# Words of the relation sums' slots made while the digits are counted; target one-hots of four slots made by one operation

## The reference

```
x = x + mean over 50000 edges (src -> dst, sorted by dst) of (norm(x) @ W + b)[src]      # neighbours
x = x + experts(norm(x)), gated by attention over 32768 other edges (4 heads, 4 experts)
x = x + relu(sum over the same 50000 edges of norm(x)[src] @ weight[relation] * edge_weight)  # relations
x = x + mixture of 8 experts, with a last layer norm
```

## Time and profile before

| what | value |
|---|---|
| median of three runs | 2875.92 us |
| profiled execution, its own time | 2869.64 us |
| its span, first to last instruction | 2867.9 us |
| mean granted TensorE clock (1 is full speed) | 0.776 |
| TensorE matmul busy | 1749.4 us, 61% |
| VectorE busy | 1312.6 us, 46% |
| GpSimd busy | 1063.5 us, 37% |
| ScalarE busy | 711.2 us, 25% |

### The profile page before, as it was taken

How to read it: one execution, slowest core, us unless ns; L and a number is a source line. 1 busy time by engine, 2 the same in 40 slices (tenths; PEclk the granted TensorE clock), 3 DMA queues, 4 the chain that set the end, 5 groups by cost and what they waited for, 6 DMA issues and landing times. The chain is left out here.

```text
span 2867.9 us, 36329 instructions
## 1 busy us (share of the span) xinstructions
PE 1749.4 (61%) x8770; PEld 1356.0 (47%) x8771; DVE 1312.6 (46%) x3820; ACT 711.2 (25%) x1568; POOL 1063.5 (37%) x1102
## 2 busy tenths in 40 slices
PE   3565577677781212399983514544555556799798
PEld 2343355455560101277762414444444446688576
DVE  7476776677740000013245604544555547522534
ACT  0001255555320000023313602222222224100222
POOL 2366555665057777200011174444444441000000
PEclk9776687877895555699986756767777768999899
DMA  4122333333221101022231632333223332233101
GB/s 151 57 73 83 85 101 102 103 105 95 59 24 25 9 8 24 20 74 94 80 122 33 195 97 78 113 97 94 88 88 95 109 96 64 88 137 113 34 1 45
DMA packets 164842, 226.19 MB, mean 79 GB/s; under 512 B 35636, under 2 KB 123990, under 8 KB 161942
## 3 DMA queue, kind: packets, MB, share of 16 engines
q0 software_dynamic: 47392, 105.58, 13.6%
q1 hardware_dynamic: 114048, 116.08, 12.9%
q10 hardware_dynamic: 3318, 3.50, 0.4%
HBM read 172.48 MB, written 105.03 MB: 97 GB/s over the span
## 5 line engine op out<-in xcount | busy, mean ns | idle before, releaser
L2018 PE MATMUL part<-coef,held 128*128 128x128 f32 x2368 | 414.1, 331 | 438.2 <-DVE window_sums L2040 188.8
L2018 PEld LDWEIGHTS part<-coef,held 128*128 128x128 f32 x2368 | 359.9, 233 | 492.5 <-DVE window_sums L2040 254.0
L456 POOL DMA_INDIRECT edge_rows<-xn_table,edge_source x391 | 372.7, 953 | 494.6 <-ACT held L2006 269.8
L456 POOL DMA_INDIRECT shared_space<-xn_table,edge_source x391 | 386.7, 989 | 317.2 <-issue 110.4
L2040 DVE SCALAR_TENSOR_TENSOR window_sums<-window_sums,fine_keep,part 128x256 f32 x592 | 284.3, 480 | 365.1 <-issue 223.7
L735 PE MATMUL part<-shared_space,hot 128*128 x832 | 315.7, 522 | 127.4 <-DVE shared_space L1087 76.9
L2006 ACT ACTIVATE held<-edge_rows 128x256 f32 x592 | 211.2, 408 | 604.8 <-remote 233.7
L1556 PE MATMUL ps_of_attention<-shared_space,W 128*128 128x320 f32 x640 | 197.0, 461 | 178.3 <-issue 177.6
L1763 DVE TENSOR_TENSOR ys<-ps_of_attention,b 128x256 f32<-128x256 f32 x100 | 41.9, 422 | 551.9 <-remote 318.5
L735 PEld LDWEIGHTS part<-shared_space,hot 128*128 128x128 f32 x832 | 192.2, 256 | 200.7 <-issue 173.8
L1410 POOL DMA_INDIRECT gall<-attention_table,attention_source x256 | 251.9, 984 | 80.0 <-issue 77.9
(11 more groups left out here) (458 smaller groups left out, 2017.4 us busy)
## 6 DMA issues: line engine op xcount, KB each, us to landing
basis_sums<-window_sums SPq DMA_DIRECT2D x74, 1024.0 KB
z<-basis_sums SPq DMA_DIRECT2D x21, 1024.0 KB, 4.8
expert_rows<-ys SPq DMA_DIRECT2D x20, 640.0 KB
shared_space<-expert_rows SPq DMA_DIRECT2D x25, 512.0 KB, 4.2
W<-in_L_ffn_W SPq DMA_DIRECT2D x20, 512.0 KB
gall<-attention_digits SPq DMA_DIRECT2D x32, 256.0 KB
xn_table<-shared_space SPq DMA_DIRECT2D x10, 640.0 KB, 4.1
shared_space<-xn_table,edge_source POOLq DMA_INDIRECT x391
```

The source lines that it names most:

```text
L456: pool.indirect_dma_start(rows[:, b % ring, 0:D], None, table, bass.IndirectOffsetOnAxis(ap=esrc[:, b:b + 1].bitcast(U32), axis=0)).then_i ...
L2018: mm = nc.tensor.matmul(part[n][:, c * P:(c + 1) * P], held[n][:, c * P:(c + 1) * P], coef[n][:, :, :].rearrange("p b w -> p (b w)"), star ...
```

## The change

1. The order of the five fine words. They are no longer made ahead of the steps. Each word is made in two halves (chunks 0 and 1, then chunks 2 and 3 of `sel`), one half at the end of each of steps 0 to 9. The words go to the PSUM banks `equal_ps` and `few_ps`.
2. VectorE makes the tables of the first three words within steps 2, 4, 5, 6 and 7. ScalarE copies the relations after the counts of 24 chunks, the weights after 30. Each operation that read 592 columns from PSUM reads 512 and 80 in two. VectorE waits for both copies before step 10, TensorE before step 11.
3. The digit one-hots lie in `low_rows` in place of over the relations and weights, so SyncE loads the first rows of digits only when all 32 chunks are counted. The line `line_j` moves to `group`.
4. Steps 0 to 9 are written out on TensorE and VectorE in place of loops; ScalarE's loop is one iteration shorter, with that iteration written out behind it.
5. `HOT = 4`: `places` makes the one-hots of four slots in one operation, after the second and the fourth set of a step, in place of two slots after each set.

```diff
-        hot = [sb(f"hot{k}", [P, SET, P]) for k in range(SETS)]
+        hot = [sb(f"hot{k}", [P, HOT, P]) for k in range(STEP // HOT)]
-        lows = [same, carried]
+        lows = low_hot
-            sp.wait_ge(digits_hot, 1)
+            sp.wait_ge(counted, CHUNKS_S)
 # ScalarE
-            with act.Fori(0, PAIRS) as ii:
+            with act.Fori(0, PAIRS - 1) as ii:
                 for k in range(2 * PER_STEP):
                     counts_of(ii * 2 * PER_STEP + k, k % 2)
+            row_copied(relf, 0)
+            for k in range(2 * PER_STEP):
+                counts_of((PAIRS - 1) * 2 * PER_STEP + k, k % 2)
+            row_copied(norm, 1)
 # TensorE
+            def fine_words(w, js):
+                of = (lambda j: moved[1][:, j, :], lambda j: spread[:, j, :], lambda j: edges.number[:, j:j + 1],
+                      lambda j: edges.rel[:, j, :], lambda j: edges.norm[:, j, :])[w]
+                rows_of = slice(0, 1) if w == 2 else slice(0, P)
+                if js[0] == 0:
+                    if w < 4:
+                        pe.wait_ge(words_used, w + 1)
+                    else:
+                        pe.wait_ge(rows_copied, 1)
+                for j in js:
+                    for lo, hi, bank in wide:
+                        mm = nc.tensor.matmul(bank[rows_of, 0:hi - lo], of(j), sel[1][:, j, lo:hi], start=(j == 0), stop=(j == EC - 1))
+                if js[-1] == EC - 1:
+                    mm.then_inc(words_ready, 1)
...
+            def counting(h):
                 for k in range(PER_STEP):
+                    c = h * PER_STEP + k
+                    yield chunk_counts(c, c % 2, first=c < 2)
+                yield fine_words(h // 2, (0, 1) if h % 2 == 0 else (2, 3))
...
-            for h in range(2):
-                step(h, counting(0, h, first=(h == 0)))
-            with pe.Fori(1, PAIRS) as ii:
-                for h in range(2):
-                    step(ii * 2 + h, counting(ii, h))
+            for h in range(2 * PAIRS):
+                step(h, counting(h))
 # VectorE
+            def counting(h):
+                if h in (2, 4, 6):
+                    (window_targets, window_groups, window_blocks)[h // 2 - 1]()
                 for k in range(PER_STEP):
                     c = h * PER_STEP + k + 2
+                    digits_of(c, c % 2)
                     yield
+                if h in (4, 5):
+                    for _ in range(6 - h):
+                        next(windows_placed)
+                if h == 7:
+                    window_landings()
+                yield
...
-                    if more:
-                        places(i + 1, k)
+                    if more and (k + 1) * SET % HOT == 0:
+                        places(i + 1, k * SET // HOT)
                     next(parts, None)
```

More of the change, by code:

```diff
@@ L950, in _ @@
             link(V.tensor_copy(fine.free[:, :], part[0:1, 0, 0:24]))
-            dve.sem_inc(words_used, 2)
-            for k in range(SETS):
+            dve.sem_inc(words_used, 1)
+            for k in range(STEP // HOT):
                 places(0, k)
[L955 to L965, removed]
@@ L966, in _ @@
-            link(V.tensor_scalar(line_j[:, :], line_i[:, :], 3, None, ALU.arith_shift_right))
-            K8 = KT // STEP
-            before, now = line_j[:, STEP - 1:KT - STEP:STEP], line_j[:, 2 * STEP - 1:KT:STEP]
-            link(V.tensor_tensor(turn[:, 1:K8], now, before, ALU.not_equal))
-            link.note(V.memset(fine.tile[:, 0:1], 0))
-            link.note(V.memset(fine.part[:, 0:1], 0))
-            link.note(V.scalar_tensor_tensor(fine.tile[:, 1:K8], before, 1.0, turn[:, 1:K8], ALU.add, ALU.mult))
@@ new lines, in window_groups, with window_places @@
+            def window_groups():
+                dve.wait_ge(words_ready, 6)
+                for lo, hi, bank in wide:
+                    link.note(V.tensor_tensor(group[:, lo:hi], bank[:, 0:hi - lo], edges.slot_iota[:, lo:hi], ALU.add))
+                link.wait()
+                dve.sem_inc(words_used, 1)
+            def window_places():
+                link(V.tensor_scalar(group[:, :], group[:, :], float(NW - 1), None, ALU.min))
+                link.note(V.memset(fine.keep[:, 0:1], 0.0))
+                link.note(V.tensor_tensor(fine.keep[:, 1:KT], group[:, 1:KT], group[:, 0:KT - 1], ALU.is_equal))
+                yield link(V.tensor_copy(line_i[:, :], group[0:1, :]))
+                link.note(V.tensor_scalar(fine.place[:, :], line_i[:, :], ZT * WT - 1, None, ALU.bitwise_and))
+                link(V.tensor_scalar(line_j[:, :], line_i[:, :], 3, None, ALU.arith_shift_right))
+                K8 = KT // STEP
+                before, now = line_j[:, STEP - 1:KT - STEP:STEP], line_j[:, 2 * STEP - 1:KT:STEP]
+                link(V.tensor_tensor(turn[:, 1:K8], now, before, ALU.not_equal))
+                yield
+                link.note(V.memset(fine.tile[:, 0:1], 0))
+                link.note(V.memset(fine.part[:, 0:1], 0))
+                link.note(V.scalar_tensor_tensor(fine.tile[:, 1:K8], before, 1.0, turn[:, 1:K8], ALU.add, ALU.mult))
+                link(V.tensor_scalar(fine.part[:, 1:K8], before, ZT - 1, None, ALU.bitwise_and))
+                yield link.note(V.tensor_scalar(fine.part[:, :], fine.part[:, :], float(WT), None, ALU.mult))
@@ new lines, in window_blocks, with window_landings @@
+            def window_blocks():
+                dve.wait_ge(words_ready, 7)
+                for lo, hi, bank in wide:
+                    link.note(V.tensor_scalar(line_i[:, lo:hi], bank[0:1, 0:hi - lo], float(EB - 1), None, ALU.min))
+                link.wait()
+                dve.sem_inc(words_used, 1)
+            def window_landings():
+                assert RING_T & (RING_T - 1) == 0
+                link.note(V.tensor_scalar(fine.ring[:, :], line_i[:, :], RING_T - 1, None, ALU.bitwise_and))
+                landings(fine.landed, KT, BLOCK_GROUPS)
+                link.wait()
@@ L1104, in _ @@
                 digits_of(c, c, first=True)
-            with dve.Fori(0, PAIRS) as ii:
-                for h in range(2):
-                    step(ii * 2 + h, parts=counting(ii, h))
+            for h in range(2 * PAIRS):
+                step(h, parts=counting(h))
+            dve.wait_ge(rows_copied, 2)
             step(COUNTED - 1)
```

62 lines of the change are left out of this document (21 added, 41 removed).

## The result

The changed kernel takes 2851.82 us (median of 5 runs, 2845.84 to 2862.23) against 2875.92 (5 runs, 2870.28 to 2880.44) for the kernel before: a ratio of 0.993, 95% interval 0.9914 to 0.9946. It is 24 us faster; 32 were forecast. The profiled execution is the slowest of its five (2862.23 us, span 2860.5), so its late stages are read with care, and a second pair of profiles stands with the experiments.

A forecast was written before the change was run, and what follows sets the result against it. No engine was busy throughout: a 47 us hole preceded the steps, VectorE bound steps 0 to 4, a three-engine chain steps 17 to 49. Terms -47.0 + 7.8 + 7 + 6 + 0.5 - 4 - 2 = -31.7 gave 2844 us, range 2824 to 2868.

The forecast's parts named there:

- halves: Steps 0 to 9: ten word halves on TensorE, partly exposed at 0.7 us each, +7 us, bounds 0 and 48.
- the hold: Before the steps: something unexplained stops TensorE for some 25 us among the fine words; called the main unknown.
- The hole goes: Ahead of the steps: VectorE goes straight from 69.1 us to the digit one-hots instead of from 116.16, -47.0 us.
- the prediction's own second point: Ahead of the steps: the five words are not worth 47 us; the first three take 12.9 us at full clock.
- the rival in which it travels with the f32 words: Steps 0 to 9: the hold returns with the f32 words beside gathers, -12 us, time 2864; chance 0.15.
- Table work into the steps: Counting steps: VectorE's fine-table work moves into them and is costed in full, +7.8 us, bounds 2 to 9.
- first steps beside gathers: Steps 0 to 4: now run beside gathers and lose between nothing and 12 us; the middle taken, +6 us.
- the rival in which the covers hold: Steps 0 to 9: tables mostly in idle time (+3), halves covered (+1), no gather loss; -51 us, time 2825; chance 0.15.
- The wait before step 10: Before step 10: VectorE's added wait for the copy of the weights costs +0.5 us, bounds 0 to 3.
- SyncE's digit rows: Loaded only after all chunks are counted, but covered by steps 11 to 16, some 90 us: cost 0.
- One-hots and written-out steps: One-hots of four slots save 0.14 us a step, -4 in all; four loop turns gone from steps 0 to 9, -2.
- The tells: Signs in the trace, such as first slot at 70 to 71 us, GpSimd's pause under 10, step 10 some 35 us earlier.

The follow-up runs named there:

- f1: Kernel before, GpSimd's gathers held back until the ninth word is made, on the second chip: 2860.87 us, ratio 1.0035 to the kernel before.
- c1_after: The changed kernel itself, unaltered, run again on the second chip: 2825.72 us, ratio 0.9919 to the kernel before.
- e5_pad_small: Changed kernel with 6 repeats of two small matmul groups early in TensorE's stream, third chip: ratio 0.9848 to the kernel before.
- e6: Changed kernel with one-hots of two slots (HOT = 2), so all of the change but the one-hots, second chip: 2837.06 us, ratio 0.9955 to before.
- e4: Kernel before with only the one-hots of four slots and the waits for them, second chip: 2843.65 us, ratio 0.9992 to before.
- e1: Kernel before, GpSimd's gathers starting only when all five fine words are made, third chip: ratio 1.0061 to the kernel before.

## Why the prediction was right, and where it was not

The time (2844 in 2824 to 2868) and the direction came out, but the time in part by luck. The sum has 21 us given back in steps 0 to 9, by table work, halves and gathers. Measured are 31.3 (109.8 to 141.1), and they have another cause: 32.2 are in step 0, from the hold, which the sum has at nothing, and the other nine steps give back none.

*The hole goes*, -47.0: measured -46.2 on the first chip and -47.1 on the second. Right. On the chips without the hold the hole is only 25.3 us, as the prediction's own second point implies: the words alone take 22 (22.0 in f1).

*The term that failed is the hold.* The prediction saw that some 25 us of the hole were no work of the words, called it the main unknown, and then let all of it vanish in the sum: it comes back only in the rival in which it travels with the f32 words (0.15). The runs show that it goes neither with the words nor away. It goes with the gathers, whose time the change does not move, and TensorE was held then both in the words and in the slots and counts of step 0. It cost +32 us (step 0: 42.1 against 9.9). The rows by which this could have been read were there: matmuls of 80 columns 2.1 us apart at full clock (86.54 and 88.64), GpSimd's fill ending at 103.9, the words speeding up from 107.5. The prediction noted the last two as evidence for the rival with the words, and did not ask what would stand in that stretch once the words were gone.

*Table work into the steps* (+7.8), *halves* (+7) and *first steps beside gathers* (+6): together +20.8 forecast. Without the hold they come to +4.7 (third chip), of which step 4 alone, with two tables in it, is 4.6 (14.3 against 9.7). On the two chips that hold, steps 1 to 9 change by -0.9 and 0.0. The halves last what was forecast (3.5, 2.3 and 4.0 us for the first three, by the rows at 111.53, 120.35 and 130.64 and those behind them), and are covered. For a loss beside gathers there is no sign: steps 1 to 4 take 43.2 us in c1_after and in e5_pad_small alike, though only in the latter do gathers run through them (30 against 14); the two are on different chips, so this is no clean comparison. The halves and the gathers belong at their lower bounds of 0, the tables at about 4.7, so the three together come near the +4 of the rival in which the covers hold. That rival's time lacked only the hold (-51 + 32 = -19, a time of 2857).

*The wait before step 10*, +0.5: the rows of both profiles of the changed kernel show none, 0; with one-hots of two slots (e6) it is 2.99, at the upper bound of 3. *SyncE's digit rows*, 0: right.

*One-hots and written-out steps*, -4 and -2. On the chips without the hold the one-hots save 0.42 us in each of the late steps, three times the 0.14 forecast, and 14.2 us in 34 of them: VectorE's own saving in its rows is 8.4 us, and the chain through it gets all of that and more, not half. On the first and second chip the late steps change by +4.9 and -1.7, and the interval of e4 (6.8 us less to 2.6 more) holds both the 4 us forecast and 0 for the one-hots alone; with the words they add 11 us, of which the runs don't say how. No run tells the -2 of the written-out steps apart from the rest.

*The tells.* First slot at 70 to 71 us (71.5): right to 0.5 us. GpSimd's pause under 10 us: wrong, 33.65, since slot 29 comes late by the hold. Step 10 some 35 us earlier: wrong, 14.9 (230.1 to 215.2). Steps 11 to 51 (first add of step 11 to the last add) changing by no more than 8 us: right on the first two chips (501.8 and 506.0, 495.1 and 496.0), not on the third (422.3 and 407.9). VectorE's idle time in steps 0 to 9 growing by over 15 us was named as what would refute the forecast, and it did grow, from 21.3 to 48.4 us, so by its own sign the mechanism was wrong though the time was in its range. The two rows are of before (120.3 to 230.1) and after (74.1 to 215.2):

```profile
120.30:230.10 109.80, 72.28 (x412) 48.40 (x411) 88.51 (x180) 11.37 (x31) 56.68 (x51) 0.73 0.21 61
```

```profile
74.10:215.20 141.10, 85.64 (x482) 52.77 (x482) 92.72 (x181) 12.69 (x35) 80.46 (x75) 0.79 0.24 70
```

The measured 24 us are thus the 46 of the hole less the 32 of the hold, and by difference some 10 from the rest, which no row of the first chip shows. On the second chip the 11.3 us between e6_words_only and c1_after are of that size, which speaks for the one-hots made together with the words.

The Trainium skill ("Runtime: NRT & Kernel Launch", Instruction fetch mechanics) says that the fetching of a long stream of instructions is mostly hidden, which bears on the written-out steps. f1_gathers_late agrees as far as it reaches: the stretch of the stream that takes 47 us beside gathers takes 22 without them, with the same instructions to fetch, and no instruction packet moves during the hold in the two rows above.

## What to carry to other kernels

When work is moved out of a gap, split the gap into the work that filled it and the time that nothing explains, and ask of the second part what it is tied to: here it ended soon after another engine's transfers, and stayed when the work had gone. An operation that starts on time in TensorE's rows may still finish 20 us late; read it by the engine that waits for its result. Moving a suspected neighbour in time (one wait on GpSimd) told in one run what moving the victim's own instructions would not, but only on a chip that shows the effect, so the kernel before is profiled beside every experiment.

## What the runs showed of the hardware

- Chips differ more than these kernels do. The same kernel before takes 2875.92, 2847.85, 2076.01 and 2077.49 us on what is called the first to the fourth chip here (the last three are certainly different ones), with mean granted clocks of 0.776 and 0.775 on the first two and 0.886 in e1's profile on the third. The change is worth 24, 22 and some 32 us (e5) on the first three.
- On the two slow ones TensorE almost stops beside the first 44 gathers, at a granted clock of 0.50 (1.2 GHz) for most of it (the clock was at full speed through the words of f1 before the gathers began, and in before until 89.6 us). The lower level does not explain it: the matmuls of before start 2.1 us apart while the clock is still 1.00, and a slot takes 1.04 us at the lower level (2.08 for two, the row at 71.52), while held ones come 5 us apart. Nor does the size of the matmuls: held ones of 80 columns (0.29 us) and of 512 (1.01 us) both start up to 2.8 us apart, and the eight of a count, of 25 columns each, end some 21 us after the slot before them (79.0 to 100.0), about 2.6 us each by estimate. What in the gathers does it, and why the 40 gathers of steps 5 to 9 do not, stays open. Late gathers and a shorter fill in the kernel after were not run on such a chip.
